# Adding the three shifted row sums of a 3x3 convolution on VectorE instead of by TensorE products

## The reference, cut to what matters

```python
def _L0_conv_ref(x, w1, b1, w2, b2, bias):
    ...
    wt = (m - a).reshape(b * c, 1, K, K)
    wt = jax.nn.softmax(wt, axis=1)
    y = lax.conv_general_dilated(xr, wt, ..., feature_group_count=b * c, ...)
    y = y + jnp.tile(bias, b)[None, :, None, None]
    return y.reshape(b, c, h, w) + x

x = x + _L0_conv_ref(_gn(x), ...)
t = _to_tokens(x)
t = t + _L1_attn_ref(_ln_t(t), ...)
t = t + _L1_ffn_ref(_ln_t(t), ...)
```

## Time and profile before

| | |
|---|---|
| median of 3 runs | 795.13 us (787.70 to 795.84) |
| the profiled execution, its own time | 789.89 us |
| its span, first to last instruction | 787.8 us |
| mean granted TensorE clock | 0.897 of 2.4 GHz |
| groups 0 to 4, ramp | 0 to about 220 us |
| groups 5, 6, 7: first burst | 221 to 245, 315 to 347, 409 to 435 us |
| groups 5, 6, 7: score stage | 245 to 268, 347 to 362, 436 to 451 us |

### The profile page before, as it was taken

One profiled execution on the slowest core, in us unless ns is written; L12 is line 12 of the kernel. 1 busy time (PEld: TensorE's weight loads), 2 busy tenths in 40 slices (PEclk: granted clock), 3 DMA queues, 4 the chain that ended last, 5 costly groups with the idle time before them and its releaser, 6 DMA issues. The chain is left out here.

```text
span 787.8 us, 14153 instructions
## 1 busy us (share of the span) xinstructions
PE 640.5 (81%) x4582; PEld 476.0 (60%) x4582; DVE 479.1 (61%) x1206; ACT 365.4 (46%) x710; POOL 368.0 (47%) x378
## 2 busy tenths in 40 slices
PE   2497989796786988798789988898886959999960
PEld 2475868575464856577466855766564737777730
DVE  2356578677267776477846776566746534556535
ACT  1143637373463535555275544654444524554420
POOL 2204141768506288654852388154834723433340
PEclk9767888788598999999999999999997989999995
DMA  2000000011144035341423234150522654555508
GB/s 84 4 15 1 15 0 15 18 52 58 53 129 148 18 103 148 103 133 37 138 85 118 85 110 143 42 165 28 175 58 92 185 156 132 168 171 163 163 6 320
DMA packets 46617, 75.50 MB, mean 96 GB/s; under 512 B 7488, under 2 KB 30048, under 8 KB 46544
## 3 DMA queue, kind: packets, MB, share of 16 engines
q1 hardware_dynamic: 35600, 57.67, 24.3%
q0 software_dynamic: 8640, 12.74, 4.7%
q10 hardware_dynamic: 2304, 4.20, 1.4%
HBM read 58.56 MB, written 16.47 MB: 95 GB/s over the span
## 5 line engine op out<-in xcount | busy, mean ns | idle before, releaser
L868 PE MATMUL bk<-xs,wbuf 64*128 64x256 f32 x1704 | 212.2, 393 | 32.8 <-DVE units L1538 18.1
L545 POOL DMA_INDIRECT expert_results<-yout,xin x142 | 140.1, 986 | 151.1 <-DVE yout L1549 107.5
L868 PEld LDWEIGHTS bk<-xs,wbuf 64*128 64x128 f32 x1704 | 162.5, 191 | 78.8 <-issue 23.9
L1538 DVE TENSOR_TENSOR units<-bk,silu 128x512 f32<-128x512 f32 x213 | 144.9, 689 | 93.3 <-ACT silu L1124 92.6
L1124 ACT ACTIVATE silu<-bk 128x512 f32<-128x512 f32 x213 | 126.4, 596 | 96.0 <-PE bk L868 95.5
L537 POOL DMA_INDIRECT expert_rows<-srow,pos x128 | 130.6, 1020 | 79.7 <-DVE pos L1483 39.1
L881 PE MATMUL bk<-units,wbuf 128*64 128x256 f32 x852 | 109.4, 393 | 1.4 <-DVE yout L1549 1.4
L881 PEld LDWEIGHTS bk<-units,wbuf 128*64 128x64 f32 x852 | 55.6, 138 | 35.3 <-issue 13.0
L1118 ACT ACTIVATE ysb<-bk 128x256 f32<-128x256 f32 x71 | 27.3, 384 | 93.9 <-PE bk L881 93.9
L492 POOL TENSOR_TENSOR rr<-vare,c_mhalf 128x16 f32<-128x16 f32 x8 | 23.5, 2936 | 80.7 <-DVE vare L1322 80.6
L1113 ACT ACTIVATE xs<-bk 128x256 f32<-128x256 f32 x71 | 27.0, 380 | 34.7 <-PE bk L825 34.7
(11 more groups left out here) (192 smaller groups left out, 982.6 us busy)
## 6 DMA issues: line engine op xcount, KB each, us to landing
wbuf<-in_weights SPq DMA_DIRECT2D x71, 576.0 KB, 3.9
xin<-expert_rows SPq DMA_DIRECT2D x71, 130.0 KB, 3.2
expert_results<-yout,xin POOLq DMA_INDIRECT x142, 3.3
xg<-in_x SPq DMA_DIRECT2D x8, 256.0 KB, 4.0
expert_rows<-srow,pos POOLq DMA_INDIRECT x128, 2.4
srow<-expert_results SPq DMA_DIRECT2D x8, 256.0 KB, 5.1
srow<-expert_results ACTq DMA_DIRECT2D x8, 256.0 KB, 6.1
out<-hid ACTq DMA_DIRECT2D x8, 256.0 KB, 5.4
```

What stands on the lines that cost most here:

```text
L545: g.indirect_dma_start(results[:, :], bass.IndirectOffsetOnAxis(ap=xin[:, t % X_SLOTS, h, ROW - 1:ROW].bitcast(U32), axis=0), yout[:, t % ...
L868: last = mm(bank[:, ch * MT:(ch + 1) * MT], wbuf[part, t % W_SLOTS, at:at + P], xs[part, t % 2, :], start=True, stop=True)
L1538: tt(units[:, t % 2, q, :], h3_ps[q], silu[:, q, :], ALU.mult).then_inc(unit_ready, 1)
```

## The change

VectorE now adds the three shifted row sums to `xres` in place, with three more chained additions of 128 x 512, once ScalarE's `add_x` is done; `conv_ready` counts behind the third. TensorE's convolution keeps one product for each (s, f), which turns the sum; its own wait for `xres_ready` goes. In a mixed iteration the row sums move from behind the second units of tile 1 to behind the first units of tile 2.

```diff
             def convolution(a, s):
                 pe.wait_ge(conv_ready, a + 1)
-                pe.wait_ge(xres_ready, 2 * a + 2)
                 if a >= MIX:
                     pe.wait_ge(ysum_ready, 2 * BURSTS[a, 0][1] - 2)
                 for f in range(2):
                     o = t_ps[:, (2 * s + f) * P:(2 * s + f + 1) * P]
                     h0 = f * HH // 2
-                    mm(o, xres[:, s, h0:h0 + 8, :], ident, start=True, stop=False)
-                    for dy in range(3):
-                        last = mm(o, hsum[:, s, h0 + dy:h0 + dy + 8, :], ident, start=False, stop=dy == 2)
+                    last = mm(o, xres[:, s, h0:h0 + 8, :], ident, start=True, stop=True)
...
                 done(tt(hin, inner[:, :, :, 0:WW], inner[:, :, :, 1:WW + 1], ALU.add))
-                tt(hin, hin, inner[:, :, :, 2:WW + 2], ALU.add).then_inc(conv_ready, 1)
+                done(tt(hin, hin, inner[:, :, :, 2:WW + 2], ALU.add))
+                dve.wait_ge(xres_ready, 2 * a + 2)
+                for dy in range(2):
+                    done(tt(xres[:, :, :, :], xres[:, :, :, :], hsum[:, :, dy:dy + HH, :], ALU.add))
+                tt(xres[:, :, :, :], xres[:, :, :, :], hsum[:, :, 2:2 + HH, :], ALU.add).then_inc(conv_ready, 1)
...
-                    if (k, q) == (1, 1):
+                    if (k, q) == (2, 0):
                         run(a, row_sums)
```

## The result

The changed kernel takes 810.19 us (median of 4 runs, 808.22 to 811.41) where the kernel before took 795.08 in runs beside them (4 runs, 787.7 to 795.84): a ratio of 1.0209, with an interval of 1.0145 to 1.0273. The medians differ by 15.1 us, and the ratio makes 16.6 of 795; 7.8 were forecast. The profiled execution took 811.41 us with a span of 809.3.

The account below looks back on a forecast made before the run. PE was busiest, but three kinds of stage were priced separately, mostly as waits between VectorE and PE. The terms summed to +7.8 us: 797.7 from the profiled 789.89, 803 from the median 795.13; range 792 to 811.

Parts of the forecast that it names:

- Group 0, -1.5: Ramp, group 0: tokens copied 4.05 us after the row sums instead of 5.56, a gain of 1.5 us that stays.
- Groups 1 and 2, -0.5 together: Ramp: scores start 1.28 us earlier but run at the lower clock, leaving gains of 0.15 and 0.35 us.
- Groups 3 and 4, +2.5 each: Ramp: additions push VectorE's next steps and PE stops twice; +2.5 us each, between +1.4 and +2.8.
- The bursts, +3.5, +3.1, +1.1: First mixed bursts of groups 5, 6, 7: the moved block of five delays tile 2's units; +3.5, +3.1, +1.1 us.
- rival (c): Clock falls in the bursts of groups 5 and 6 too; with the ramp's bounds +11.8 us, 806.9; chance 0.15.
- The score stages, -1.9, -0.5, -0.5: Score stages of groups 5, 6, 7: shorter convolution brings scores and rden forward; -1.9, -0.5, -0.5 us.
- (d): All eight groups: additions contend with POOL's SBUF reads, up to 1.06 us each, +8.5 on top; 811.4; chance 0.04.
- (b): Not slower: additions run in VectorE's idle time and the shorter convolution sets the scores; -9.5 us, 785.6; chance 0.05.
- (a): Bursts: tiles hide most of the block, groups 5 and 6 cost 1.1 us each; +3.4, 793.3 or 798.5; chance 0.24.

Follow-up runs that it names:

- e9: Kernel before with the 12 hsum products of every group left out and nothing in their place; 786.20 us, ratio 0.9908.
- e6: Kernel before plus VectorE's three additions in groups 0 to 4 into a tile nobody reads, TensorE not waiting for them; 791.53 us, ratio 1.0002.
- e10: Kernel before plus three unread additions in groups 0 to 4, the convolution waiting for the last, all products kept; 805.72 us, ratio 1.0167.
- e2: Kernel before with the change in groups 5 to 7 alone, row sums moved as in the change; 798.39 us, ratio 1.0091.
- e4: Changed kernel plus 6 dummy TensorE products ahead of the wait for the additions in groups 1 to 4; 809.81 us, 1.0217 of the kernel before.
- e8: Changed kernel plus 6 dummy products in groups 1 to 4 and four more before n2's turn in groups 3 and 4; 808.68 us, 1.021 of before.
- e11: Kernel before with the change in groups 0 and 5 alone, group 5's additions placed ahead of wtok; 786.92 us, ratio 0.9936.

## Why the prediction was wrong

The sign and the stops of TensorE that were forecast were right, the size was not: the forecast was +7.8 us, and 15.1 to 16.6 were measured. Point by point:

- **Group 0, -1.5.** Right: the tokens are copied at 22.48 where 22.2 was forecast, and 23.69 before.

```profile
22.48 0.60 ACT L1026 ACTIVATE tok<-bk 128x512 f32<-128x512 f32 x1 [4.82 <-PE bk L653]
```

  To the row sums of group 1 the gain is 1.3 to 2.5 us.
- **Groups 1 and 2, -0.5 together, bounds 0 and -1.28 each.** This is the step that failed first. Group 1 can't be told: the time from its row sums to the next x<-u,att is 22.95 us in place of 24.31, and 23.1 to 25.8 where its code is as before. The stretch of group 2 lost 4.7 us, outside both bounds. I had written that "the long convolution is what PE does while the clock is low", which e9 and e6 confirm, and then priced its absence at about 0.8 us a score step. The runs put in its place a clock that stays at 0.50 through scores, fc1 and part of the attention, up to about 97.5 us, and a mean of 0.66 over the stretch.
- **Groups 3 and 4, +2.5 each, upper bound +2.8.** The upper bound took VectorE's push as the most that could be lost. VectorE's queue alone costs 1.3 and 1.6 (e6), close to my lower bound of 1.4; the stretches lost 7.5 and 3.5. The term that was mis-sized is the clock: without the products 4.4 and 3.0 (e9), and the stop on top of it (e10).
- **The bursts, +3.5, +3.1, +1.1.** The place and the sign were right. Against unchanged code (31.0, some 36.8, some 31.0) the changed kernel has +5.9, +3.2 and +0.4. Group 5 is the one that was mis-sized: its two stops are 3.67 us together, 3.2 more than the 0.46 of before and near the 3.5 forecast; the other 2.7 lie behind the second, where the clock is down, rival (c)'s mechanism. Group 6's two stops are 6.78 us in place of 3.52, 3.3 more, near the 3.1 forecast.
- **The score stages, -1.9, -0.5, -0.5.** -1.0 for group 5, and +1.3 and -0.4 against the profile of before. In groups 5 and 6 the clock is lower than before (0.73 and 0.91, against 0.86 and 1.00 in the windows of these stages); e2, with the same code, has 16.7 for group 6, so its +1.3 is not the change's alone.
- **The rivals.** (d) is out: 692 ns for the mean addition at both lines. (The row of 1.75 us that gave its price is a multiplication of two SBUF tensors on VectorE, not an addition.) (b) is out: the kernel became slower, and in group 3 TensorE, being ready, waited 1.15 us for VectorE's third addition. (a) is out in group 5. (c) was the nearest, and it took the clock for an extra of 1.7 us a time, not for the main term.

So the failing step is one: I priced the clock as a delay of the first scores, and left it at its old level everywhere else. It was the products themselves that TensorE did in the time at 0.50, and taking them away left that time to products on the chain, and made it longer. Worked out from the lengths and mean clocks of group 3's stretch, with two levels: some 6 us of it are at 0.50 in the kernel before, 24 in the changed kernel and 22 in e9. That the loss goes with the clock is shown (e9, e10, and e4 and e8 in both directions); why the clock stays down is not. The Trainium skill, "TensorE: Matmul & The Clock Gate", section "What's actually happening", says that the array's clock is seen in two states, 1.2 and 2.4 GHz. The traces agree: their clock records hold 0.50 and 1.00 and nothing between.

## What to carry to other kernels

Before you take products off TensorE, look at the granted clock of the stretch they stand in: at 0.50 they may cost nothing, and without them what stands behind may run at 0.50, and for longer. Price such a change from a kernel that leaves the products out with nothing in their place; here that accounts for 9.3 of the 15.7 us lost in the ramp, which have nothing to do with the engine that took the work over. A block on an engine with a fixed order is priced by the wait that it lies in: here five instructions behind a wait cost 5.9 us, and nothing measurable where the last three of them lie inside it.

## What the runs showed of the hardware

That leaving work out can make a stretch longer: e9's three stretches, 89.6 us with 412 TensorE records, where the kernel before has 80.3 us with 486. That TensorE can be busy without a gap in the profile for 12 us (118 to 130 in e9) and stay at a granted clock of 0.50, while in e8 it came to 1.00 at the end of the second run of dummy products (0.55 in the window from 124 to 130, 1.00 in the one behind it). That a granted clock of 1.00 early in a trace can be the lack of a record: the lengths of the products tell (2.07 us for eight of them in e11, 2.08 in the kernel before at 0.50). And that one kernel's runs scatter by 1% with the mean clock: 0.904 at 787.05 us and 0.889 at 795.72.
